# Second layer's experts: gated rows stored in slot order and gathered by token, expert number read ahead of the transposes

## The reference, cut to what matters

```python
gate_scores = softmax(einsum('btd,ed->bte', x, Wg))
topk_val, topk_idx = top_k(gate_scores, 2)
topk_val = topk_val / (topk_val.sum(-1, keepdims=True) + 1e-9)
comb = (one_hot(topk_idx, 8) * topk_val[..., None]).sum(-2)
for e in range(8):
    h = einsum('btd,hd->bth', x, W1[e]) + b1[e]     # 256 -> 1024
    a, b = split(h, 2, axis=-1)
    g = a * sigmoid(b)                              # 512 wide: the "gated row"
    eo = einsum('bth,dh->btd', g, Wo) + bo          # 512 -> 256, one Wo for all experts
    out = out + eo * comb[..., e:e + 1]
```

## Time and profile before

| | us |
|---|---|
| median of 3 runs | 1906.9 (1899.91 to 1917.9) |
| profiled execution | 1913.12 |
| its span, first to last instruction | 1911.4 |
| PE busy in the span | 1592.3 (83%) |
| POOL busy in the span | 851.5 (45%) |

### The profile page before, as it was taken

The page is one execution under the profiler, slowest core; times in us unless marked ns, Lnnn a source line. Parts: engine busy times, 40 slices in busy tenths (PEclk is TensorE's granted clock), DMA queues, the critical chain, the costliest instruction groups (busy, mean ns, idle before and its releaser), DMA issues. The chain is left out here.

```text
span 1911.4 us, 48579 instructions
## 1 busy us (share of the span) xinstructions
PE 1592.3 (83%) x16482; PEld 1180.4 (62%) x16483; DVE 1067.3 (56%) x2274; ACT 812.3 (42%) x1574; POOL 851.5 (45%) x1177
## 2 busy tenths in 40 slices
PE   5999999999962999995989898888888249898868
PEld 4777777777741666664777677777777124343356
DVE  3666666666634222222576666767676556655545
ACT  3667666676640222222555454545554001111111
POOL 3666666666630111113455555545554116666500
PEclk8999999999975999997998888989898559999979
DMA  4112121100005111112112111211100202222255
GB/s 120 52 54 74 52 74 52 30 29 21 23 12 208 33 33 33 33 30 80 31 60 72 54 50 54 73 31 33 29 27 10 98 29 89 90 93 89 84 181 175
DMA packets 51897, 119.22 MB, mean 62 GB/s; under 512 B 10221, under 2 KB 28629, under 8 KB 48501
## 3 DMA queue, kind: packets, MB, share of 16 engines
q1 hardware_dynamic: 40948, 88.42, 14.2%
q0 software_dynamic: 10880, 29.90, 4.8%
HBM read 89.32 MB, written 28.97 MB: 62 GB/s over the span
## 5 line engine op out<-in xcount | busy, mean ns | idle before, releaser
L959 DVE TENSOR_REDUCE a_mx<-a_SM 100x2 bf16<-100x722 f32 x384 | 351.3, 915 | 193.1 <-PE a_SM L425 187.6
L704 ACT ACTIVATE a_Pr<-a_ST 120x1600 f32<-120x1600 f32 (+3 forms) x192 | 225.0, 1172 | 77.4 <-PE a_ST L457 75.9
L425 PE MATMUL a_SM<-a_KT,a_QM 32*100 32x362 f32 x768 | 159.0, 410 | 112.8 <-DVE a_mx L959 108.5
L753 POOL TENSOR_TENSOR a_rstd<-a_ve,a_powers 100x1 f32<-100x1 f32 x192 | 123.2, 642 | 278.3 <-DVE a_ve L929 274.9
L1717 PE MATMUL g_PH<-w,g_xT 128*128 x456 | 211.3, 607 | 20.4 <-issue 16.5
L467 PE MATMUL a_M<-a_Pr,a_V 120*32 120x100 f32 (+3 forms) x4608 | 187.9, 263 | 0.6 <-ACT a_Pr L704 0.6
L425 PEld LDWEIGHTS a_SM<-a_KT,a_QM 32*100 32x100 f32 x768 | 63.8, 162 | 180.5 <-DVE a_mx L959 149.2
L467 PEld LDWEIGHTS a_M<-a_Pr,a_V 120*32 120x32 f32 (+3 forms) x4608 | 145.7, 125 | 27.0 <-issue 23.2
L1717 PEld LDWEIGHTS g_PH<-w,g_xT 128*128 128x128 f32 x456 | 82.7, 191 | 115.0 <-issue 115.0
L1764 ACT ACTIVATE g_sg<-g_ab 128x512 f32<-128x512 f32 x57 | 35.9, 630 | 217.6 <-DVE g_ab L1792 205.9
L355 PE MATMUL a_M<-a_ch,a_wkh 128*128 128x362 f32 x256 | 101.6, 397 | 29.0 <-POOL a_cl L821 29.0
(11 more groups left out here) (204 smaller groups left out, 3707.5 us busy)
## 6 DMA issues: line engine op xcount, KB each, us to landing
w<-in_E_w SPq DMA_DIRECT2D x24, 1024.0 KB, 6.7
a_ct<-in_ctx SPq DMA_DIRECT2D x64, 362.0 KB, 3.0
g_GR<-gated_rows SPq DMA_DIRECT2D x32, 400.0 KB
keep_rows<-a_keep SPq DMA_DIRECT2D x64, 100.0 KB
tile_rows<-e_y SPq DMA_DIRECT2D x32, 128.0 KB, 1.7
b_rows<-in_E_b SPq DMA_DIRECT2D x1, 4096.0 KB
out<-g_y SPq DMA_DIRECT2D x32, 100.0 KB
X<-in_x SPq DMA_DIRECT2D x1, 2800.0 KB
```

The source lines that it names most:

```text
L425: last = nc.tensor.matmul(SM[0:LQ, half, 0:LKP], QM[b.p][rows, chunk, m, :], KT[b.p][rows, chunk, :], start=True, stop=True)
L704: nc.scalar.activation(Pr[0:n, s, :].rearrange("p (r q) -> p r q", r=GROUPS), ST[0:n, :, 0:PER * LQ], ACT.Exp, scale=SCALE).then_inc(exp_d ...
L753: nc.gpsimd.tensor_tensor(rstd[k][:], ve[k][:].to_broadcast([LQ, n]), powers[:, 0:n], ALU.pow).then_inc(rstd_ready[k], 1)
L959: V_.tensor_reduce(pair, SM[0:LQ, :, 0:LK], AX_X, ALU.max).then_inc(max_done, 1)
```

## The change

The first phase no longer scatters. SP stores each `hs` with a plain transfer at the tile's own place, row j*128 of `gated`, which is now 57*128 rows in slot order. The second phase fetches by token: for each sequence POOL issues two indirect gathers of 100 rows of 2 KB, one for each choice, with column b of `slots[k]` as row numbers, straight from the tile that routing made. GR is 8 buffers for one sequence each (the same bytes as before). `pairs`, `spare` and what made them are gone; in both layers' routing the matmul of line 1219 is 2*NT columns wide, not 3*NT. On PE the expert number is read ahead of `rows(j + 1)` and not between it and `up(j)`.

```diff
@@ routing
-                    last = nc.tensor.matmul(PS[:, 2, 0:3 * NT], in_row[k][:, b, :],
-                                            in_tile[k][:, b].rearrange("q a j -> q (a j)"),
+                    last = nc.tensor.matmul(PS[:, 2, 0:2 * NT], in_row[k][:, b, :],
+                                            in_tile[k][:, b, 0:2].rearrange("q a j -> q (a j)"),
...
-                link(V_.scalar_tensor_tensor(tok_f[:], PS[:, 2, NT:2 * NT], float(NB), seq_f[:], ALU.mult, ALU.add))
-                link(V_.scalar_tensor_tensor(pair_f[:], second[:], float(TOK - NB), tok_f[:], ALU.mult, ALU.add))
...
-            if layer == 1:
-
-                link(V_.tensor_scalar(seq_f[:], PS[:, 2, 2 * NT:3 * NT], -1.0, 1.0, ALU.mult, ALU.add))
-                link(V_.tensor_scalar(seq_f[:], seq_f[:], spare[:], None, ALU.mult))
-                link(V_.tensor_tensor(env["pairs"][:, 0:NT], seq_f[:], pair_f[:], ALU.add))
@@ gated_tiles, SP
-            def load(r):
-                if r == 0:
-                    sp.wait_ge(g_stored[0], 16 * ((NT + 1) // 2))
-                    sp.wait_ge(g_stored[1], 16 * (NT // 2))
-                if r >= DEEP:
-                    sp.wait_ge(comb_ready, ROUND * (r - DEEP + 1))
-                for k in range(2):
-                    rows = t["gated"][k * TOK:(k + 1) * TOK, :].rearrange("(q b) f -> q b f", b=NB)
-                    sp.dma_start(GR[r % DEEP][:, k], rows[:, ROUND * r:ROUND * (r + 1), :]
-                                 ).then_inc(g_loaded[r % DEEP], 16)
+            def store(j, p):
+                sp.wait_ge(h_ready, j + 1)
+                sp.dma_start(t["gated"][bass.ds(j * 128, 128), :], hs[p][:]).then_inc(g_stored[p], 16)
...
-            for r in range(DEEP):
-                load(r)
+            with sp.Fori(0, NT // 2) as i:
+                for p in range(2):
+                    store(i * 2 + p, p)
+            for j in range(NT // 2 * 2, NT):
+                store(j, j % 2)
             for b in range(NB):
-                if b % ROUND == 0 and 1 <= b // ROUND <= ROUNDS - DEEP:
-                    load(b // ROUND - 1 + DEEP)
                 sp.wait_ge(y_ready, b + 1)
@@ gated_tiles, POOL
-            def scatter(j, p, r, first):
-                pool.wait_ge(h_ready, j + 1)
-                if not first:
-                    pool.wait_ge(g_stored[1 - p], r * 16 + 16 * p)
...
-                nc.gpsimd.tensor_copy(sidx[p][:], env["pairs"][:, bass.ds(j, 1)]).then_inc(sidx_ready, 1)
-                pool.wait_ge(sidx_ready, j + 1)
-                pool.sem_inc(turns, 1)
-                nc.gpsimd.indirect_dma_start(t["gated"], bass.IndirectOffsetOnAxis(sidx[p][:], 0), hs[p][:], None
-                                             ).then_inc(g_stored[p], 16)
+            def pair_of_rows(b):
+                if b >= RING:
+                    pool.wait_ge(comb_ready, b - RING + 1)
+                for k in range(2):
+                    nc.gpsimd.indirect_dma_start(GR[b % RING][:, k], None, t["gated"],
+                                                 bass.IndirectOffsetOnAxis(env["slots"][k][:, b:b + 1], 0)
+                                                 ).then_inc(g_loaded[b % RING], 16)
...
+            for j in range(NT // DEEP * DEEP, NT):
+                gather(j, j % DEEP, False)
+            pool.wait_ge(g_stored[0], 16 * ((NT + 1) // 2))
+            pool.wait_ge(g_stored[1], 16 * (NT // 2))
+            for b in range(NB):
+                pair_of_rows(b)
@@ gated_tiles, PE
-            def up(j, p, low):
-                e = expert_of(pe, j)
+            def up(j, e, p, low):
                 pe.wait_ge(xT_ready, j + 1)
...
                 for p in range(DEEP):
+                    e = expert_of(pe, i * DEEP + p)
                     rows(i * DEEP + (p + 1), (p + 1) % DEEP, i + (p + 1) // DEEP, False)
-                    up(i * DEEP + p, p % 2, 2)
+                    up(i * DEEP + p, e, p % 2, 2)
@@ gated_tiles, DVE
             def combine(b):
-                r, k = b // ROUND, b % ROUND
-                dve.wait_ge(g_loaded[r % DEEP], 32 * (r // DEEP + 1))
+                rows = GR[b % RING]
+                dve.wait_ge(g_loaded[b % RING], 32 * (b // RING + 1))
...
-                V_.tensor_scalar(part[:], GR[r % DEEP][:, 1, k, :], env["share"][1][:, b:b + 1], None, ALU.mult
+                V_.tensor_scalar(part[:], rows[:, 1, :], env["share"][1][:, b:b + 1], None, ALU.mult
                                  ).then_inc(part_ready, 1)
```

More of the change, by code:

```diff
@@ L1571, in gated_tiles @@
     G = GH // 128
-    ROUND = 2
     DEEP = 4
-    ROUNDS = NB // ROUND
+    RING = 8
     tag = "g1_"
@@ L1589, in gated_tiles @@
         gidx = [sb(f"gidx{p}", [128, 1], I32) for p in range(DEEP)]
-        sidx = [sb(f"sidx{p}", [128, 1], I32) for p in range(2)]
         xs = [sb(f"xs{p}", [128, D]) for p in range(DEEP)]
@@ L1595, in gated_tiles @@
         hs = [sb(f"hs{p}", [128, GH]) for p in range(2)]
-        GR = [sb(f"GR{p}", [LQ, 2, ROUND, GH]) for p in range(DEEP)]
+        GR = [sb(f"GR{p}", [LQ, 2, GH]) for p in range(RING)]
         part = sb("part", [LQ, GH])
@@ L1619, in gated_tiles @@
         ssum_ready = sem("ssum_ready")
-        g_loaded = [sem(f"g_loaded{p}") for p in range(DEEP)]
+        g_loaded = [sem(f"g_loaded{p}") for p in range(RING)]
         part_ready = sem("part_ready")
@@ L1672, in gather @@
                                              ).then_inc(rows_loaded[p], 16)
-            def scatter(j, p, r, first):
-                pool.wait_ge(h_ready, j + 1)
-                if not first:
-                    pool.wait_ge(g_stored[1 - p], r * 16 + 16 * p)
-                pool.sem_inc(turns, 1)
-                nc.gpsimd.tensor_copy(sidx[p][:], env["pairs"][:, bass.ds(j, 1)]).then_inc(sidx_ready, 1)
-                pool.wait_ge(sidx_ready, j + 1)
-                pool.sem_inc(turns, 1)
-                nc.gpsimd.indirect_dma_start(t["gated"], bass.IndirectOffsetOnAxis(sidx[p][:], 0), hs[p][:], None
-                                             ).then_inc(g_stored[p], 16)
+            def pair_of_rows(b):
[5 more added lines that the diff above has]
+                                                 ).then_inc(g_loaded[b % RING], 16)
             for j in range(DEEP):
                 gather(j, j, True)
-            for j in range(DEEP, 2 * DEEP):
-                gather(j, j % DEEP, False)
-                scatter(j - DEEP, j % 2, (j - DEEP) // 2, j == DEEP)
-            with pool.Fori(2, NT // DEEP) as i:
+            with pool.Fori(1, NT // DEEP) as i:
                 for p in range(DEEP):
                     gather(i * DEEP + p, p, False)
-                    scatter(i * DEEP + (p - DEEP), p % 2, i * 2 + (p // 2 - 2), False)
-            for j in range(NT // DEEP * DEEP, NT + DEEP):
-                if j < NT:
-                    gather(j, j % DEEP, False)
-                scatter(j - DEEP, j % 2, (j - DEEP) // 2, False)
+            for j in range(NT // DEEP * DEEP, NT):
[4 more added lines that the diff above has]
+                pair_of_rows(b)
         @block.tensor
@@ L1722, in _ @@
             for j in range(DEEP):
+                e = expert_of(pe, j)
                 rows(j + 1, (j + 1) % DEEP, (j + 1) // DEEP, False)
-                up(j, j % 2, j)
+                up(j, e, j % 2, j)
             with pe.Fori(1, (NT - 1) // DEEP) as i:
                 for p in range(DEEP):
+                    e = expert_of(pe, i * DEEP + p)
                     rows(i * DEEP + (p + 1), (p + 1) % DEEP, i + (p + 1) // DEEP, False)
-                    up(i * DEEP + p, p % 2, 2)
+                    up(i * DEEP + p, e, p % 2, 2)
             for j in range((NT - 1) // DEEP * DEEP, NT):
+                e = expert_of(pe, j)
                 if j + 1 < NT:
                     rows(j + 1, (j + 1) % DEEP, (j + 1) // DEEP, False)
-                up(j, j % 2, 2)
+                up(j, e, j % 2, 2)
             def turn(b):
@@ L1842, in combine @@
                     dve.wait_ge(gT_ps, b - 1)
-                V_.scalar_tensor_tensor(comb[b % 2][:], GR[r % DEEP][:, 0, k, :], env["share"][0][:, b:b + 1], part[:],
+                V_.scalar_tensor_tensor(comb[b % 2][:], rows[:, 0, :], env["share"][0][:, b:b + 1], part[:],
                                         ALU.mult, ALU.add).then_inc(comb_ready, 1)
@@ L1864, in program @@
     t["keep"] = nc.dram_tensor("keep_rows", (TOK, D), F32, kind="Internal").ap()
-    t["gated"] = nc.dram_tensor("gated_rows", (2 * TOK + 128, GH), F32, kind="Internal").ap()
+    t["gated"] = nc.dram_tensor("gated_rows", (NT1 * 128, GH), F32, kind="Internal").ap()
     t["out_rows"] = t["out"].rearrange("b q d -> (b q) d")
@@ L1877, in program @@
         tile_e = sb("tile_e", [128, NTMAX], I32)
-        pairs = sb("pairs", [128, NTMAX], I32)
         pool_turns = ctx.enter_context(nc.semaphore("pool_turns"))
         env = {"pool_turns": pool_turns, "X": X, "aff": affs, "alpha": alpha, "share": share,
```

(5 more changed lines are left out.)

6 lines of the change are left out of this document (1 added, 5 removed).

## The result

The changed kernel takes 1899.9 us in the median (1895.8 to 1906.5, 20 runs), the kernel before 1911.1 beside it (20 runs): ratio 0.995, 95% interval 0.993 to 0.997. That is a gain of 11 us, clear of zero but inside the 1% that counts as no change, where 45 were forecast and a time of 1862. The profiled spans are 1901.8 and 1911.4.

The account below looks back on a forecast made before the run. POOL was taken to bound the first phase, ten transfer engines the second. With -35.4 (first phase), -7.8 (between phases) and gathers 1.15 us apart the end was 1867.9; routing's -1.8 gave 1866.1, median 1862, range 1852 to 1882.

Parts of the forecast that it names:

- The first phase: First phase: with the scatter off POOL, PE binds at 3.665 us per tile, last transposes at 1770.1; -35.4 us.
- Routing: Routing stage: five DVE steps gone, -1.3 us, and a narrower list matmul, taken as 0.5 us; sum -1.8 us.
- Expert number: First phase on PE: reading it ahead of the transposes gains nothing, up to 0.45 us per tile if rows were late.
- Between the phases: From DVE's last product to the first `part`: 7.7 us in place of 15.5, -7.8 us.
- The spacing p: Second phase: distance between POOL's indirect gathers, from 0.99 to 1.85 us, taken as 1.15 us.
- End = 1795.4 + 63p: Second phase: end of the span if POOL's 64 gathers set the pace; 1867.9 with 1.15, before routing's gain.
- (b): Second phase: POOL's queue time doesn't overlap, gathers 1.85 us apart, end 1910.2, no change; chance 0.09.
- (d): First phase: doesn't speed up, as something else needs 4.35 us per tile; -35 lost, median 1897; chance 0.04.
- The cause of the stalls of before: Second phase of before: transfers on ten of 16 engines, always full, limit it to 227 GB/s; 5 us reach PE.
- The two rules: Second phase: DVE instructions can hold POOL's transfers; GpSimd transfers take ten engines from a moving start, lifting the 227 GB/s limit.
- rival (a): Second phase: `part` holds POOL for 0.48 us per sequence, gathers 1.39 us apart, median 1877; chance 0.20.

Follow-up runs that it names:

- e7: The kernel before with POOL's loop unrolled and the two index copies and their waits gone; 1878.9 us, ratio 0.985.
- e9: The changed kernel with the expert number read where it was before, between row transposes and matmuls; 1900.3 us, ratio 0.995.
- e1: The changed kernel with its 64 gathers replaced by plain loads of 100 consecutive rows issued by SyncE, not the tokens' rows; 1865.2 us, ratio 0.979.
- e13: The changed kernel with its gathers replaced by 128 plain POOL loads of 50 rows, without a pause, not the tokens' rows; 1861.3 us, ratio 0.977.
- e11: The changed kernel with a POOL copy of the slot column, waited for, ahead of each of the 64 gathers; 1929.8 us, ratio 1.011.
- e8: The kernel before without index copies, token order sequence x 100 + token, second phase by plain SyncE loads of 100 consecutive rows; 1870.9 us, ratio 0.981.
- e14: The changed kernel with one small POOL copy, not waited for, ahead of each of the 64 gathers; 1896.7 us, ratio 0.995.
- e2: The changed kernel with its 64 gathers replaced by plain POOL loads of 100 consecutive rows, not the tokens' rows; 1860.9 us, ratio 0.977.
- e10: The changed kernel with each of the 64 gathers fetching 48 rows and not 100; 1903.2 us, ratio 0.995.
- e12: The changed kernel with no index copies in the first phase and two extra unread gathers per tile there; 1961.7 us, ratio 1.027.
- e6: The changed kernel with each sequence's second gather replaced by a plain SyncE load of 100 consecutive rows, not the tokens' rows; 1865.7 us, ratio 0.977.

## Why the prediction was wrong

**The first phase: right.** Forecast 3.665 us per tile to the end and last transposes at 1770.1; measured 3.65 and 3.66 in turn and 1767.7, of which 1.0 was already won ahead of the phase. First to last product 36.3 us shorter (forecast 35.4). SP, DVE and the store bound nothing. That POOL's queue was the bound, and not the matmuls, is also what e7 shows, which gains the same by the removal of the copies alone.

**Routing: better than forecast, by a term taken too small.** The start of the experts can't be compared between profiles, as the parts ahead differ by up to 16 us. From the second batch of list matmuls on, which begins 0.06 us after the same DVE step in both, it can. Timelines of after, then one row of before; the batch of before is in the earlier trace rows:

```profile
1552.59 3.22 PE L1217 MATMUL r_PS<-r_in_tile,r_in_row 100*128 100x114 bf16 x32 [7.83 <-DVE r_in_tile L1310]
...
1558.75 0.19 POOL L1650 COPY g_gidx<-toks 128x1 int32<-128x1 int32 x1 [56.09 <-POOLq L102]
```

```profile
1559.90 0.19 POOL L1668 COPY g_gidx<-toks 128x1 int32<-128x1 int32 x1 [59.15 <-POOLq L102]
```

From the batch to POOL's first copy of the experts it is 9.00 us before and 6.16 after: 2.8 won, not 1.8. The batch takes 3.22 us in place of 4.77, which is the full third (1.6) where 0.5 was taken, and the DVE steps give the forecast 1.3. This is 1.0 in the gain's favour and no part of the miss.

**Expert number: right**, nothing (e9).

**Between the phases: right.** 7.6 us from the end of the last product (1776.53 + 0.69) to the first `part`, forecast 7.7, before 15.5.

**The spacing p: mis-sized by little.** Forecast 1.15, measured 1.30 (1.00 busy, 0.30 of queue time that does not overlap). With it the formula gives 1795.4 + 63 x 1.30 - 1.8 = 1875.5, a median of 1871, inside the range. The two bounds, 0.99 and 1.85, held it.

**The step that failed** is "End = 1795.4 + 63p": that the second phase takes the longer of POOL's pace and PE's 2.08 per sequence. It left out that the one can act on the other. The end is 1901.8 and not 1875.5; the 26.3 us between come with PE's late increments and the low clock that follows the waits. With nothing late, and rows in time, e1 and e13 need 74.7 and 75.2 us from the first `part` to the end; after needs 116.9. None of the rivals had this: (b) and (d) gave about the time measured, but (b)'s regular 0.56 between gathers is 0.30, and (d)'s slow first phase is not there: that they come near the time is chance.

Nothing in the profile of before could show it by itself, since there the 0.83 us gap and the copy stand between any two indirect transfers; e7 and e11 are clean with such a gap, or with a rest behind each pair. What could have been seen is that the change enters a state that no row had shown (64 such transfers in a row), and that the range should have had a case for what that does to others, and not to POOL alone.

**The cause of the stalls of before was half right.** The text said that ten engines, always full at 227 GB/s, bound that phase. The share of 0.64 is the same in e1, but the rate is 239, and 247 in e8 at 0.66. So 227 is what the loads of before reach, not a limit of ten engines. That error cost nothing in the sum.

**The two rules.** On DVE holding POOL: rival (a)'s mechanism is there, and `comb` has it too. In after a gather that starts inside `part` takes up to 1.24 us (1787.35) and one that starts inside `comb` up to 1.45 (1849.68), in place of 1.00; in e14 1.26 (1803.83) and 1.45. The held ones end 0.85 to 0.89 us after the DVE instruction has ended; a gather that starts together with `part`, within 0.03 us, is not held (1805.17, 1.00). Rival (a) asked for 0.24 on each of the 64 and the mean is 1.03, so it is real and small; in e14, where gathers fall inside `comb` more often, the mean is 1.12. The Trainium skill (SBUF — State Buffer, "Who interferes with whom") agrees in that there is such a hold. The same section says "PE and ACT never wait on anyone." By the matmuls' own rows the trace agrees, a product group takes its usual 1.73 us at the granted clock of 1.00; but ACT waited 8.7 us for an increment, and of increments the section says nothing.

The DMA share is 0.68 in e2 and 0.77 in e13, where POOL issues the plain loads, against 0.64 by SyncE in e1; 0.77 of 16 engines is 12.3, more than ten. That goes with the Trainium skill (DMA: Bandwidth & Descriptors, "Why a DMA increments its semaphore by 16 and not by 1"), by which transfers of GpSimd spread over the engines; it changed no time here, as e1 and e2 both run at PE's pace.

## What to carry to other kernels

When a change puts transfers on an engine's queue without anything between them, ask what a dense stream does to the others' handshakes, and try the stream alone before counting its pace: look for waits whose producer had long ended. Run it long enough: here the first ten to thirteen gathers of a stream cost nothing. Indirect transfers by POOL are best kept apart, with plain transfers for whatever order can be prepared by a scatter beforehand; e8 does all of the computation that way and beats both kernels. And where an engine is bound by small copies of indices ahead of its transfers, point the transfer at the column itself (e7) before moving work to other engines.

## What the runs showed of the hardware

- Increments of TensorE's semaphores came up to 12.0 us after the work in the profile of after and 19.2 us in e10, while POOL issued indirect gathers 1.17 to 1.31 us apart; in both phases (e12), with 48, 100 or 128 rows, consecutive or scattered. They came on time with POOL's plain transfers 0.5 us apart (e13), with indirect ones that had about 1 us of rest (e6, e11) or a rest behind each two (e7), and with one 0.20 us copy between, at 1.40 us and more (e14). DVE's and ACT's increments showed no such delay: PE starts transposes at most 0.15 us after the `comb` or `gT` that it needs, in after as in the clean kernels.
- The delay needs a run-up. In the second phase of the seven kernels that have it, the first late increment belongs to PE work that ended 13 to 16 us after the first gather, behind 11 to 13 gathers; in the first phase of e12, behind ten. It looks like something that fills up and drains when POOL rests, but by what path this happens is not shown, nor whether e14 is clean for the copy or for the longer distance. In after and e14 alike the trace also lacks the records of many increments, of DVE and ACT too, which it has in full in e1 and e2; whether the recording has a part in the delay was not tried.
- An indirect transfer of 100 rows costs POOL 1.00 us and 0.30 of queue time; from start to start it is 1.30 with 100 rows, 1.25 with 128 and 1.17 with 48. A plain one takes 0.51 to 0.56 without idle time.
- A gather that starts inside a DVE instruction with `tensor_scalar` or with two SBUF inputs ends 0.85 to 0.89 us after that instruction, up to 0.45 late (after, e14).
- The granted clock fell to 0.50 in several stretches of after's second phase (mean 0.76 from 1795 to 1845) once PE stood between groups, and a product group took 3.4 to 3.6 us there in place of 1.73. This lengthens the loss: PE's transposes and products of the second phase sum to 93.3 us in after and 79.0 in e1, so by estimate the clock makes at most 14 us of it.
